# The first layer of the experts by Strassen's seven products of tiles instead of eight

## The chip, the cores and the metric
The kernel runs on one core of a Trainium2 chip. The metric is the time of the whole program on the device in microseconds (us), the median of three runs. A core has TensorE (PE; its weight loads are listed as PEld), VectorE (DVE), ScalarE (ACT), GpSimd (POOL) and SyncE (SP), which run apart and wait for each other by semaphores.

## The reference, cut to what matters
The program is one decoder layer on 64 x 256 tokens of 256 features: self-attention, cross-attention, then a block with another attention and a mixture of eight experts. The change touches the experts alone. Each takes up to a quarter of the 16384 tokens, 4096 rows:

```python
h = jax.nn.relu(jnp.einsum('ecd,edf->ecf', buf, w1) + b1[:, None, :])
y = (jnp.einsum('ecf,efd->ecd', h, w2) + b2[:, None, :]) * (1.0 - MOE_TOKEN_DROPOUT)
```

with `buf` 8 x 4096 x 256, `w1` 8 x 256 x 1024 and `w2` 8 x 1024 x 256, all in fp32. The rows of `y`, each times its gate, are added to the tokens they came from.

## The kernel before, in words
The parts of the program run one after the other: `prepare`, three calls of `attention`, `route`, `dispatch`, and `experts`, which fills the last third of the time. `experts` works in chunks of 512 rows, eight chunks to an expert and 64 in all; `k` (0 or 1) is the set of buffers of an expert, `par` (0 or 1) that of a chunk, `n` the chunk's number. There is no scheduler: each engine has its own list of instructions, written out in the source, and waits for counts of semaphores.

For a chunk, POOL gathers 512 rows from memory (`gather`, L1546), three chunks ahead. TensorE transposes them in eight pieces into two PSUM tiles `turn` (`turn_rows`, L1450), and VectorE copies these to `xT`, features on the partitions, two halves of 128 features by 512 rows (L1496). Then TensorE makes the eight tiles of the first layer: for each `f`, 128 of the 1024 hidden features, two matmuls with 512 columns, one for each half of the input features, are summed in PSUM (`hid`, two buffers, L1466). ScalarE reads each with the bias and ReLU into `hT` (L1488). After the eight tiles and the transposes of the next chunk, TensorE makes the second layer: four groups of 128 rows, each a sum of eight matmuls with 256 columns (`res`, L1476), for which a tile of `hT` is the loaded operand. VectorE scales them and adds the bias (`y`, L1532), multiplies by the gate (`gated`, L1540), and POOL adds each quarter to the output in memory by an indirect DMA (L1566), one after another: each waits until the one before it has landed.

At the first chunk of an expert VectorE waits for the weights and spreads the biases (L1511 to L1518), for which ScalarE waits (L1485). The weights of expert `e + 2` are asked for by SP when expert `e` is done (L1436).

Of the kernel before, what the change touches and what calls it, by code (L numbers as in the profile page):

```python
# [8 lines left out]
P = 128  # L9
# [1143 lines left out]
NE = 8  # L1153
# [214 lines left out]
def experts(nc, C, D, io, scratch, out):  # L1368
# [7 lines left out]
    with ExitStack() as ctx:  # L1376
# [14 lines left out]
        turn = [ps(f"turn{i}", [P, NS]) for i in range(2)]  # L1391
        hid = [ps(f"hid{i}", [P, NS]) for i in range(2)]
# [3 lines left out]
        (turned, xT_ready, hid_full, hid_read, res_full, res_read, biases, gated_ready, added, chosen, cleared, listed) = (sem(n) for n in (  # L1396
            "turned", "xT_ready", "hid_full", "hid_read", "res_full", "res_read", "biases", "gated_ready", "added", "chosen",
            "cleared", "listed"))
# [22 lines left out]
        with nc.Block() as block:  # L1421
# [20 lines left out]
            @block.tensor  # L1442
            def _(pe):
                def turn_rows(r, j, n):
                    xb, use = x_turn(r, j)
                    pe.wait_ge(x_in[xb], 64 * use + 64)
                    need(pe, xT_ready, 2 * n)
                    for a in range(2):
                        for t in range(4):
                            last = nc.tensor.transpose(turn[a][:, t * P:(t + 1) * P], x[xb][:, t, a * P:(a + 1) * P],  # L1450
                                                       C["ident_f"][:, :])
                        last.then_inc(turned, 1)

                turn_rows(0, 0, 0)
                for r in ends_apart(pe):
                    for e, k, c, par, n, j in chunks(r):
                        if c == 0:
                            pe.wait_ge(w_in[k], 48 * r + 48)
                        pe.wait_ge(xT_ready, 2 * n + 2)
                        for f in range(NF):  # L1460
                            m = NF * n + f
                            if k or c or f >= 2:
                                need(pe, hid_read, m - 1)
                            h = hid[f % 2]
                            for a in range(2):
                                last = nc.tensor.matmul(h[:, :], w1[k][:, a, f * P:(f + 1) * P], xT[par][:, a, :],  # L1466
                                                        start=a == 0, stop=a == 1)
                            last.then_inc(hid_full, 1)
                        if another(n):
                            turn_rows(r, j + 1, n + 1)  # L1470
                        pe.wait_ge(hid_read, NF * n + NF)
                        for t in range(2):
                            need(pe, res_read, 2 * n)
                            for s in range(2):
                                for f in range(NF):
                                    last = nc.tensor.matmul(res[t][:, s, :], hT[par][:, f, (2 * t + s) * P:(2 * t + s + 1) * P],  # L1476
                                                            w2[k][:, f, :], start=f == 0, stop=f == NF - 1)
                            last.then_inc(res_full, 1)

            @block.scalar  # L1480
            def _(act):
                for r in rounds(act, NE // 2):
                    for e, k, c, par, n, j in chunks(r):
                        if c == 0:
                            act.wait_ge(biases, 2 * e + 2)  # L1485
                        for f in range(NF):
                            act.wait_ge(hid_full, NF * n + f + 1)
                            nc.scalar.activation(hT[par][:, f, :], hid[f % 2][:, :], ACT.Relu, bias=b1[k][:, f:f + 1])\  # L1488
                                .then_inc(hid_read, 1)

            @block.vector
            def _(dve):
                def copy_rows(n, par):
                    for a in range(2):
                        dve.wait_ge(turned, 2 * n + a + 1)
                        nc.vector.tensor_copy(xT[par][:, a, :], turn[a][:, :]).then_inc(xT_ready, 1)  # L1496

                def list_tokens(r, j, n):
                    nc.vector.tensor_copy(token[j % (2 * XB)][:, :], C["token"][:, bass.ds(4 * n, 4)]).then_inc(listed, 1)

                for t in x:
                    nc.vector.memset(t[:, :, :], 0.0).then_inc(cleared, 1)  # L1502
                for n in range(XB - 1):
                    list_tokens(0, n, n)
                copy_rows(0, 0)
                for r in ends_apart(dve):
                    for e, k, c, par, n, j in chunks(r):
# [3 lines left out]
                        if c == 0:  # L1511
                            dve.wait_ge(w_in[k], 48 * r + 48)
                            nc.vector.tensor_copy(b1[k][:, :], C["b1"][:, bass.ds(e * NF, NF)]).then_inc(biases, 1)
                            nc.vector.tensor_copy(rank[k][:, :], C["ranks"][:, bass.ds(e, 1)])
                            for s in range(2):
                                last = nc.vector.tensor_scalar(b2s[k][:, s, :], b2[k][:, :], 0.8, None, ALU.mult)
                            last.then_inc(biases, 1)
                            dve.wait_ge(biases, 2 * e + 2)  # L1518
                        if another(n):
                            copy_rows(n + 1, 1 - par)  # L1520
                        tail = x[j % XB]
                        nc.vector.scalar_tensor_tensor(first[par][:, :, :], tail[:, :, 258:259], rank[k][:, :],
# [155 lines left out]
```

## Time and profile before
| | before |
|---|---|
| median of 3 runs | 5969.68 us (5968.39 to 5971.0) |
| the profiled execution | 5964.57 us, its span 5962.9 us |
| mean granted TensorE clock | 0.984 |
| busy share of the span: PE, PEld, DVE, ACT, POOL | 94, 68, 62, 52, 34% |

Times in the trace are counted from the span's start. A matmul in fp32 leaves two records, each with its own weight load, so the two matmuls of a tile of `hid` are four records. The end of a matmul's record is modelled and reaches past the start of the next one, so the pace of TensorE is read from start to start and not from the mean duration.

### The profile page before, as it was taken

To read this page: it belongs to the slowest core of one execution; us is meant where nothing else is said; L and a number is where in the kernel's file an instruction comes from. 1 tells how busy PE (TensorE), PEld (TensorE's weight loads), DVE (VectorE), ACT (ScalarE), POOL (GpSimd) and SP (SyncE) were. 2 spreads that over 40 slices of the span, in tenths; PEclk is the share of its full clock that TensorE was granted. 3 is DMA by queue.
4 is the path that set the end of the run, shared out by engine and by line. 5 is a ranking of instruction groups with operands and counts; after the bars stand their busy time and mean duration, and the time that the engine had idled before them with its cause. 6 is when DMAs were issued, how large, how long until landed. Compare 5 with 4: busy or idle time off the path is not lost. (4 is left out here: it accounts for less than half of the span.)

```text
span 5962.9 us, 144169 instructions
## 1 busy us (share of the span) xinstructions
PE 5621.1 (94%) x44441; PEld 4031.8 (68%) x44441; DVE 3721.2 (62%) x10169; ACT 3120.9 (52%) x6803; POOL 2036.6 (34%) x1753
## 2 busy tenths in 40 slices
PE   0999999989999999799999999958999999999998
PEld 0677777667777777577777777734666666666666
DVE  7888888778888887688888888875111111111111
ACT  4788888746666666477777777635121111211111
POOL 0322222233333333244444444401333333333332
PEclk9999999989999999999999999979999999999999
DMA  5777777556666665466766666631222222222221
GB/s 157 178 184 182 182 185 180 148 159 175 174 173 173 174 174 166 120 178 170 182 171 175 177 170 181 168 26 49 39 53 51 33 49 53 32 45 51 38 39 20
DMA packets 625511, 750.10 MB, mean 126 GB/s; under 512 B 131075, under 2 KB 554188, under 8 KB 625328
## 3 DMA queue, kind: packets, MB, share of 16 engines
q1 hardware_dynamic: 568992, 679.62, 43.7%
q0 software_dynamic: 49152, 63.10, 6.6%
q10 hardware_dynamic: 7184, 5.00, 0.3%
q8 instruction: 108, 1.77, 0.1%
q14 instruction: 75, 0.61, 0.0%
HBM read 476.49 MB, written 272.24 MB: 126 GB/s over the span
## 5 line engine op out<-in xcount | busy, mean ns | idle before, releaser
L1488 ACT ACTIVATE exp_hT<-exp_hid,exp_b 128x512 f32<-128x512 f32 x512 | 351.8, 687 | 1487.3 <-PE exp_hid L1466 1372.3
L1476 PE MATMUL exp_res<-exp_w,exp_hT 128*128 128x256 f32 x4096 | 901.2, 381 | 0.8 <-ACT exp_hT L1488 0.8
L1466 PE MATMUL exp_hid<-exp_xT,exp_w 128*128 128x512 f32 x2048 | 891.0, 593 | 0.9 <-DVE exp_xT L1496 0.9
L1476 PEld LDWEIGHTS exp_res<-exp_w,exp_hT 128*128 128x128 f32 x4096 | 773.8, 190 | 112.2 <-ACT exp_hT L1488 1.6
L1566 POOL DMA_INDIRECT out_dram<-exp_gated,exp_token x256 | 406.1, 1586 | 1099.4 <-issue 412.7
L931 DVE TENSOR_REDUCE F_tops<-F_score 128x2 f32<-128x512 f32 x1024 | 684.3, 686 | 59.8 <-PE F_score L685 40.8
L822 ACT ACTIVATE F_probs<-F_scoreT 128x512 f32<-128x512 f32 x1024 | 583.8, 590 | 236.8 <-PE F_scoreT L654 236.8
L1466 PEld LDWEIGHTS exp_hid<-exp_xT,exp_w 128*128 128x128 f32 x2048 | 389.8, 191 | 464.6 <-issue 458.5
L1496 DVE COPY exp_xT<-exp_turn 128x512 f32<-128x512 f32 x128 | 82.6, 686 | 803.2 <-PE exp_turn L1450 803.2
L931 DVE TENSOR_REDUCE A_tops<-A_score 128x3 f32<-128x384 f32 x1024 | 531.6, 554 | 62.3 <-PE A_score L671 54.0
L1532 DVE SCALAR_TENSOR_TENSOR exp_y<-exp_res,exp_b2s 128x512 f32<-128x512 f32 x128 | 88.5, 692 | 735.4 <-PE exp_res L1476 735.4
L822 ACT ACTIVATE A_probs<-A_scoreT 128x384 f32<-128x384 f32 x1024 | 451.0, 488 | 23.1 <-PE A_scoreT L642 14.7
L654 PE MATMUL F_scoreT<-QS,KS 98*128 98x256 bf16 x2048 | 365.4, 275 | 9.7 <-ACT F_probs L822 1.5
L685 PE MATMUL F_score<-KS,QS 96*128 96x256 bf16 x2048 | 362.7, 274 | 8.3 <-DMA KS<-d_k 7.4
L931 DVE TENSOR_REDUCE X_tops<-X_score 128x4 f32<-128x484 f32 x512 | 329.8, 658 | 29.0 <-PE X_score L680 28.9
L822 ACT ACTIVATE X_probs<-X_scoreT 121x512 f32<-121x512 f32 x512 | 295.1, 595 | 78.3 <-PE X_scoreT L650 72.6
L1547 POOL DMA_INDIRECT exp_x<-d_h,exp_token x256 | 269.1, 1051 | 195.6 <-DMA exp_w<-in_L_ffn_w_dram 117.9
L666 PE MATMUL A_score<-causal,ident_b 128*128 128x256 bf16 x1024 | 282.8, 276 | 12.1 <-DMA KS<-d_k 8.3
L638 PE MATMUL A_scoreT<-ident_b,causal 128*128 128x128 bf16 x2048 | 286.1, 221 | 3.2 <-ACT A_probs L822 1.1
L669 PE MATMUL A_score<-KS,QS 96*128 96x256 bf16 x1024 | 281.2, 275 | 0.0
L711 PE MATMUL F_outs<-F_probs,V 128*32 128x256 f32 x4096 | 275.4, 387 | 1.9 <-ACT F_outT L831 1.9
L642 PE MATMUL A_scoreT<-QS,KS 98*128 98x256 bf16 x1024 | 277.2, 271 | 0.0
(330 smaller groups left out, 12099.1 us busy)
## 6 DMA issues: line engine op xcount, KB each, us to landing
QS<-d_q SPq DMA_DIRECT2D x384, 192.0 KB, 3.6
KS<-d_k SPq DMA_DIRECT2D x256, 192.0 KB, 4.0
QS<-d_q SPq DMA_DIRECT2D x384, 128.0 KB, 3.9
KS<-d_k SPq DMA_DIRECT2D x256, 128.0 KB, 4.0
d_q<-A_q_parts SPq DMA_DIRECT2D x64, 384.0 KB, 3.6
d_k<-A_k_parts SPq DMA_DIRECT2D x64, 384.0 KB, 3.9
QS<-d_q SPq DMA_DIRECT2D x384, 64.0 KB, 3.7
d_q<-X_q_parts SPq DMA_DIRECT2D x64, 384.0 KB, 4.0
```

The costliest lines, as they stand in the source:

```text
L638: mm(s[:, n * P:(n + 1) * P], C["causal"][:, 0:P], ident_b[:, :], start=n == 0, stop=False, skip_group_check=True)
L642: last = mm(s[:, P:384], k[0:98, i, 0:P], q[0:98, i, :], start=False, stop=True, skip_group_check=True)
L654: last = mm(s[:, n * 256:(n + 1) * 256], k[0:98, i, n * P:(n + 1) * P], q[0:98, i, :], start=True, stop=True)
L666: mm(s[:, 0:384].rearrange("p (n k) -> p n k", n=3)[:, 0:3:2, :], ident_b[:, :], C["causal"][:, :].rearrange("p (n k) -> p n k", n=2), sta ...
L669: mm(s[:, P:384], q[0:96, i, P:256], k[0:96, i, :], start=False, stop=False, skip_group_check=True)
L685: last = mm(s[:, n * 256:(n + 1) * 256], q[0:96, i, n * P:(n + 1) * P], k[0:96, i, :], start=True, stop=True)
L822: nc.scalar.activation(probs[m % 2][0:KR, at:at + HB, :].rearrange("p u x -> p (u x)"), scoreT[i % TB][0:KR, 0:HB * TCOL], ACT.Exp)\
L931: nc.vector.tensor_reduce(dst, src, AX.X, ALU.max).then_inc(score_read, 1)
L1466: last = nc.tensor.matmul(h[:, :], w1[k][:, a, f * P:(f + 1) * P], xT[par][:, a, :], start=a == 0, stop=a == 1)
L1476: last = nc.tensor.matmul(res[t][:, s, :], hT[par][:, f, (2 * t + s) * P:(2 * t + s + 1) * P], w2[k][:, f, :], start=f == 0, stop=f == NF - 1)
L1488: nc.scalar.activation(hT[par][:, f, :], hid[f % 2][:, :], ACT.Relu, bias=b1[k][:, f:f + 1])\
L1566: nc.gpsimd.indirect_dma_start(out, bass.IndirectOffsetOnAxis(token[j % (2 * XB)][:, s:s + 1], 0), gated[par][:, s, :], None, bounds_check ...
```

## The change
The product of the first layer is cut into blocks, two by two: the weights into input half by output half (hidden features `u` and `u + 4`, in tiles of 128, for `u` from 0 to 3), the rows of the chunk into two halves of 256. Of the eight products of blocks, seven sums and differences are multiplied instead (Strassen's scheme in Winograd's form). The sums of the rows (`xTs`, `mix_rows`) are made by VectorE once a chunk, those of the weights (`w1s`, `fold_weights`) once an expert, in the last but one chunk of the expert before it, with the spreading of the biases. Each `u` then has seven matmuls with 256 columns. `lead` gets one product and later a second one on top; ScalarE copies it out after each (`lone`, `pair`). `corner` gets one. `side` gets two, one in each half of its bank, and VectorE reads both (`joined`, `side_read`) before `close` adds the last two. VectorE puts the four quarters of the two hidden tiles into `hT` by additions; ScalarE then applies bias and ReLU in place (`rectify`). The second layer's matmuls are the same 32, in an order by pairs of tiles, each with its own wait; the transposes are made in two groups of four with one `turn` buffer. PSUM holds one tile each of `turn` and `corner`, two each of `lead`, `side` and `res`. The buffers of Q, K and V, which `experts` does not use, are given back ahead of it.

```diff
+        HR, HF = NS // 2, NF // 2
+        w1s = [sb(f"w1s{i}", [P, 4, 512]) for i in range(2)]
+        xTs = [sb(f"xTs{i}", [P, 4, HR]) for i in range(2)]
+        lone, pair, both = [[sb(f"{n}{i}", [P, HR]) for i in range(2)] for n in ("lone", "pair", "both")]
+        turn = ps("turn", [P, NS])
+        lead = [ps(f"lead{i}", [P, HR]) for i in range(2)]
+        corner = ps("corner", [P, HR])
+        side = [ps(f"side{i}", [P, 2, HR]) for i in range(2)]
...
+        BY_PAIR = [f for u in range(HF) for f in (u, u + HF)]
...
+                        def close(u):
+                            s = side[u % 2]
+                            pe.wait_ge(side_read, HF * n + u + 1)
+                            mm(s[:, 0, :], ws(3, u), xT[par][:, 1, HR:NS], start=False, stop=True, skip_group_check=True)
+                            mm(s[:, 1, :], w(1, u + HF), xs(3), start=False, stop=True, skip_group_check=True).then_inc(closed, 1)
+
+                        def products(t, s, fs, begin):
+                            for f in fs:
+                                pe.wait_ge(hid_read, NF * n + BY_PAIR.index(f) + 1)
+                                last = mm(res[t][:, s, :], hT[par][:, f, (2 * t + s) * P:(2 * t + s + 1) * P], w2[k][:, f, :],
+                                          start=begin and f == fs[0], stop=f == BY_PAIR[-1], skip_group_check=True)
+                            return last
+
...
+                        for u in range(HF):
+                            l, s = lead[u % 2], side[u % 2]
+                            need(pe, pair_kept, HF * n + u - 1)
+                            mm(l[:, :], w(0, u), xT[par][:, 0, 0:HR], start=True, stop=False, skip_group_check=True)                                .then_inc(led, 1)
+                            need(pe, corner_read, HF * n + u)
+                            mm(corner[:, :], w(1, u), xT[par][:, 1, 0:HR], start=True, stop=True).then_inc(cornered, 1)
+                            if u == 0:
+                                pe.wait_ge(mixed, 4 * n + 4)
+                                if c == 0:
+                                    pe.wait_ge(folded, 4 * e + 4)
+                            need(pe, summed, 2 * HF * n + 2 * u - 2)
+                            mm(s[:, 0, :], ws(0, u), xs(0), start=True, stop=False, skip_group_check=True)
+                            mm(s[:, 1, :], ws(2, u), xs(2), start=False, stop=False, skip_group_check=True)
+                            if u:
+                                close(u - 1)
+                            pe.wait_ge(led_kept, HF * n + u + 1)
+                            mm(l[:, :], ws(1, u), xs(1), start=False, stop=True, skip_group_check=True).then_inc(sided, 1)
+                        need(pe, res_read, 2 * n)
+                        products(0, 0, BY_PAIR[0:4], True)
+                        close(HF - 1)
+                        products(0, 0, BY_PAIR[4:6], False)
                         if another(n):
+                            rows_here(r, j + 1)
+                            turn_half(j + 1, n + 1, 0)
+                        products(0, 1, BY_PAIR[0:6], False)
+                        products(0, 0, BY_PAIR[6:8], False)
+                        products(0, 1, BY_PAIR[6:8], False).then_inc(res_full, 1)
+                        if another(n):
+                            turn_half(j + 1, n + 1, 1)
+                        products(1, 0, BY_PAIR, True)
+                        products(1, 1, BY_PAIR, True).then_inc(res_full, 1)
...
+                        def rectify(u):
+                            for i in (2 * u, 2 * u + 1):
+                                f = BY_PAIR[i]
+                                act.wait_ge(summed, NF * n + i + 1)
+                                nc.scalar.activation(hT[par][:, f, :], hT[par][:, f, :], ACT.Relu, bias=b1[k][:, f:f + 1])\
+                                    .then_inc(hid_read, 1)
+                        for u in range(HF):
+                            act.wait_ge(led, HF * n + u + 1)
+                            need(act, corner_read, HF * n + u - 1)
+                            nc.scalar.activation(lone[u % 2][:, :], lead[u % 2][:, :], ACT.Copy).then_inc(led_kept, 1)
+                            if u > 1:
+                                rectify(u - 2)
+                            act.wait_ge(sided, HF * n + u + 1)
+                            need(act, summed, NF * n + 2 * u - 2)
+                            nc.scalar.activation(pair[u % 2][:, :], lead[u % 2][:, :], ACT.Copy).then_inc(pair_kept, 1)
+                        rectify(HF - 2)
+                        rectify(HF - 1)
...
+                def copy_half(n, par, a):
+                    dve.wait_ge(turned, 2 * n + a + 1)
+                    v.tensor_copy(xT[par][:, a, :], turn[:, :]).then_inc(xT_ready, 1)
+                    dve.wait_ge(xT_ready, 2 * n + 2)
+                    v.tensor_tensor(m[:, 0, :], b12, b11, ALU.subtract).then_inc(mixed, 1)
+                    v.tensor_tensor(m[:, 2, :], b22, b12, ALU.subtract).then_inc(mixed, 1)
+                    dve.wait_ge(mixed, 4 * n + 1)
+                    v.tensor_tensor(m[:, 1, :], b22, m[:, 0, :], ALU.subtract).then_inc(mixed, 1)
+                    dve.wait_ge(mixed, 4 * n + 3)
+                    v.tensor_tensor(m[:, 3, :], b21, m[:, 1, :], ALU.subtract).then_inc(mixed, 1)
+                def fold_weights(e, k, use):
+                    dve.wait_ge(w_in[k], 48 * use + 48)
+                    v.tensor_tensor(m[:, 0, :], a21, a22, ALU.add).then_inc(folded, 1)
+                    v.tensor_tensor(m[:, 2, :], a11, a21, ALU.subtract).then_inc(folded, 1)
...
+                def first_corner(n, par, u):
+                    dve.wait_ge(cornered, HF * n + u + 1)
+                    dve.wait_ge(led_kept, HF * n + u + 1)
+                    v.tensor_tensor(hT[par][:, u, 0:HR], corner[:, :], lone[u % 2][:, :], ALU.add).then_inc(corner_read, 1)
...
+                fold_weights(0, 0, 0)
+                spread_biases(0, 0)
+                copy_half(0, 0, 0)
+                copy_half(0, 0, 1)
+                mix_rows(0, 0)
+                first_corner(0, 0, 0)
...
+                        for u in range(HF):
+                            s, p, b = side[u % 2], pair[u % 2], both[u % 2]
+                            dve.wait_ge(pair_kept, HF * n + u + 1)
+                            v.tensor_tensor(b[:, :], s[:, 0, :], p[:, :], ALU.add).then_inc(joined, 1)
+                            dve.wait_ge(joined, HF * n + u + 1)
+                            v.tensor_tensor(hT[par][:, u + HF, HR:NS], s[:, 1, :], b[:, :], ALU.add).then_inc(side_read, 1)
+                            if u < HF - 1:
+                                first_corner(n, par, u + 1)
+                            dve.wait_ge(closed, HF * n + u + 1)
+                            v.tensor_tensor(hT[par][:, u, HR:NS], s[:, 0, :], p[:, :], ALU.add).then_inc(summed, 1)
+                            v.tensor_tensor(hT[par][:, u + HF, 0:HR], s[:, 1, :], p[:, :], ALU.add).then_inc(summed, 1)
                         if another(n):
+                            copy_half(n + 1, 1 - par, 0)
...
+                        if c == NC - 2 and not (k and isinstance(r, int) and r == NE // 2 - 1):
+                            fold_weights(e + 1, 1 - k, r + k)
+                            spread_biases(e + 1, 1 - k)
+                        if another(n):
+                            copy_half(n + 1, 1 - par, 1)
+                            mix_rows(n + 1, 1 - par)
+                        dve.wait_ge(biases, 2 * e + 2)
...
+                            if t == 1 and another(n):
+                                first_corner(n + 1, 1 - par, 0)
...
-            "QS": [sb(f"QS{i}", [98, H, 256], BF16) for i in range(2)],
-            "KS": [sb(f"KS{i}", [98, H * 256], BF16) for i in range(2)],
-            "V": [sb(f"V{i}", [P, 2, H, VW]) for i in range(2)], "xmean": sb("xmean", [P, 2 * B]), "xrstd": sb("xrstd", [P, 2 * B]),
...
+        with ExitStack() as stacks:
+            sb, _, _ = allocators(nc, stacks, "")
+            C["QS"] = [sb(f"QS{i}", [98, H, 256], BF16) for i in range(2)]
+            C["KS"] = [sb(f"KS{i}", [98, H * 256], BF16) for i in range(2)]
+            C["V"] = [sb(f"V{i}", [P, 2, H, VW]) for i in range(2)]
+            prepare(nc, C, D, io)
+            attention(nc, C, D, io, scratch, "A")
...
```

On TensorE one chunk before, from its first to its last matmul, is:

```order
L1466 MATMUL exp_hid<-exp_xT,exp_w 128x512 x16
L1450 MATMUL exp_turn<-ident_f,exp_x 128x128 x8
L1476 MATMUL exp_res<-exp_w,exp_hT 128x256 x32
```

Now the pair `u = 2` (its lines are alike for 1 and 3), and the first part of the second layer behind `u = 3`:

```order
L1499 MATMUL exp_lead<-exp_xT,exp_w 128x256
L1501 MATMUL exp_corner<-exp_xT,exp_w 128x256
L1507 MATMUL exp_side<-exp_xTs,exp_w1s 128x256
L1508 MATMUL exp_side<-exp_xTs,exp_w1s 128x256
L1483 MATMUL exp_side<-exp_xT,exp_w1s 128x256
L1484 MATMUL exp_side<-exp_xTs,exp_w 128x256
L1512 MATMUL exp_lead<-exp_xTs,exp_w1s 128x256
...
L1489 MATMUL exp_res<-exp_w,exp_hT 128x256 x4
L1483 MATMUL exp_side<-exp_xT,exp_w1s 128x256
L1484 MATMUL exp_side<-exp_xTs,exp_w 128x256
L1489 MATMUL exp_res<-exp_w,exp_hT 128x256 x2
```

Four other matmuls stand between L1512 of a pair and the two that close it (L1483, L1484). On VectorE nothing of the first layer stood before between two `y`; now each pair has (buffer numbers behind the names; `exp_side0` is the pair's own `side`, `corner` and `lone1` those of the pair behind it):

```order
L1619 TENSOR_TENSOR exp_both0<-exp_side0,exp_pair0 128x256
L1621 TENSOR_TENSOR exp_hT1<-exp_side0,exp_both0 128x256
L1594 REGISTER_ALU
L1596 TENSOR_TENSOR exp_hT1<-exp_corner,exp_lone1 128x256
L1625 TENSOR_TENSOR exp_hT1<-exp_side0,exp_pair0 128x256
L1626 TENSOR_TENSOR exp_hT1<-exp_side0,exp_pair0 128x256
```

The last two wait for `closed`, the first for ScalarE's copy `pair`; the next pair's L1619 stands right behind them.

## Rows read from the trace of the kernel before
**Rows 1.** The page: busy time, and the lines of the last chain.
```profile
PE 5621.1 (94%) x44441; PEld 4031.8 (68%) x44441; DVE 3721.2 (62%) x10169; ACT 3120.9 (52%) x6803; POOL 2036.6 (34%) x1753
...
PE exp_res L1476 15%; PE exp_hid L1466 15%; PE exp_turn L1450 1%; DMA out_dram<-exp_gated,exp_token 0%; DMA exp_x<-d_h,exp_token 0%; DVE exp_x L1502 0%; POOL out_dram L1566 0%; POOL exp_x L1547 0%; DVE exp_xT L1496 0%; DVE exp_y L1532 0%; ACT exp_hT L1488 0%; DVE exp_gated L1540 0%; POOLq L1547 0%; POOLq L1566 0%; POOLq L32 0%
```
**Rows 2.** One stretch of `experts`: span; busy PE, PEld, DVE, ACT, POOL; clock, DMA, GB/s.
```profile
4300.00:5900.00 1600.00, 1600.00 (x5822) 1069.61 (x5821) 261.59 (x698) 307.49 (x448) 587.29 (x446) 1.00 0.24 43
```
**Rows 3.** TensorE in order of time: start, duration, group of records.
```profile
5204.41 13.90 PE L1466 MATMUL exp_hid<-exp_xT,exp_w 128*128 128x512 f32 x32
5218.14 1.04 PE L1450 MATMUL exp_turn<-ident_f,exp_x 128*128 128x128 f32 x8
5219.09 14.08 PE L1476 MATMUL exp_res<-exp_w,exp_hT 128*128 128x256 f32 x64
5233.00 13.90 PE L1466 MATMUL exp_hid<-exp_xT,exp_w 128*128 128x512 f32 x32
```
**Rows 4.** Costliest groups: busy time, mean ns of one, idle before.
```profile
L1476 PEld LDWEIGHTS exp_res<-exp_w,exp_hT 128*128 128x128 f32 x4096 | 773.8, 190 | 112.2 <-ACT exp_hT L1488 1.6
L1488 ACT ACTIVATE exp_hT<-exp_hid,exp_b 128x512 f32<-128x512 f32 x512 | 351.8, 687 | 1487.3 <-PE exp_hid L1466 1372.3
L1532 DVE SCALAR_TENSOR_TENSOR exp_y<-exp_res,exp_b2s 128x512 f32<-128x512 f32 x128 | 88.5, 692 | 735.4 <-PE exp_res L1476 735.4
L831 ACT ACTIVATE X_outT<-X_outs 128x256 f32<-128x256 f32 x256 | 97.8, 382 | 110.6 <-PE X_outs L706 110.4
L1050 DVE TENSOR_TENSOR F_tok<-F_work,F_rec 128x256 f32<-128x256 f32 x128 | 54.3, 424 | 4.4
L1236 DVE TENSOR_TENSOR route_hit<-route_hit,route_down 128x1024 f32<-128x1024 f32 x2 | 2.4, 1224 | 0.1
```
**Rows 5.** Experts, in order of time, ScalarE, VectorE and POOL; idle before in brackets.
```profile
5204.61 0.69 DVE L1532 SCALAR_TENSOR_TENSOR exp_y<-exp_res,exp_b2s 128x512 f32<-128x512 f32 x1 [5.39 <-PE exp_res L1476]
5204.93 1.59 POOL L1566 DMA_INDIRECT out_dram<-exp_gated,exp_token  x1 [1.69 <-DMA out_dram<-exp_gated,exp_token]
5205.34 0.77 DVE L1540 TENSOR_SCALAR exp_gated<-exp_y,exp_gate 128x256 f32<-128x256 f32 x2
5206.33 0.69 ACT L1488 ACTIVATE exp_hT<-exp_hid,exp_b 128x512 f32<-128x512 f32 x1 [15.89 <-PE exp_hid L1466]
5214.34 1.59 POOL L1566 DMA_INDIRECT out_dram<-exp_gated,exp_token  x1 [1.67 <-DMA out_dram<-exp_gated,exp_token]
5228.88 1.59 POOL L1566 DMA_INDIRECT out_dram<-exp_gated,exp_token  x1 [11.59 <-issue]
```
**Rows 6.** The last chunk: ScalarE's last tile and the matmuls that wait for it.
```profile
5933.15 0.69 ACT L1488 ACTIVATE exp_hT<-exp_hid,exp_b 128x512 f32<-128x512 f32 x1 [1.03 <-PE exp_hid L1466]
5933.89 14.08 PE L1476 MATMUL exp_res<-exp_w,exp_hT 128*128 128x256 f32 x64 [0.78 <-ACT exp_hT L1488]
5941.18 0.69 DVE L1532 SCALAR_TENSOR_TENSOR exp_y<-exp_res,exp_b2s 128x512 f32<-128x512 f32 x1 [19.90 <-PE exp_res L1476]
```
**Rows 7.** Other stages: VectorE behind itself, order of time and costliest groups.
```profile
3291.43 0.26 DVE L1049 RECIPROCAL F_rec<-F_work 128x16 f32<-128x16 f32 x1 [0.61 <-PE F_work L785]
3291.72 0.42 DVE L1050 TENSOR_TENSOR F_tok<-F_work,F_rec 128x256 f32<-128x256 f32 x1
3292.06 0.68 DVE L931 TENSOR_REDUCE F_tops<-F_score 128x2 f32<-128x512 f32 x1
...
3301.47 0.18 DVE L990 BATCH_NORM_AGGREGATE F_umean_var<-F_ustats 128x2 f32<-128x6 f32 x1 [0.15 <-DVE F_ustats L986]
```
**Rows 8.** The first chunk, in order of time.
```profile
4113.33 1.97 PE L1450 MATMUL exp_turn<-ident_f,exp_x 128*128 128x128 f32 x8 [18.28 <-DMA exp_x<-d_h,exp_token]
4115.34 0.69 DVE L1496 COPY exp_xT<-exp_turn 128x512 f32<-128x512 f32 x1 [0.16 <-PE exp_turn L1450]
4116.18 15.43 PE L1466 MATMUL exp_hid<-exp_xT,exp_w 128*128 128x512 f32 x32 [0.88 <-DVE exp_xT L1496]
```
**Rows 9.** Who waited for whom in `experts`, TensorE: us in total, times, longest.
```profile
PE exp_turn L1450 <- DMA exp_x<-d_h,exp_token: 18.3, 1, 18.3
PE exp_hid L1466 <- DVE exp_xT L1496: 0.9, 1, 0.9
PE exp_res L1476 <- ACT exp_hT L1488: 0.8, 1, 0.8
```

More of the change, by code:

```diff
@@ L1443, in _, with turn_half, rows_here @@
             def _(pe):
-                def turn_rows(r, j, n):
+                mm = nc.tensor.matmul
+                def turn_half(j, n, a):
+                    need(pe, xT_ready, 2 * n + a)
+                    for t in range(4):
+                        last = nc.tensor.transpose(turn[:, t * P:(t + 1) * P], x[j % XB][:, t, a * P:(a + 1) * P],
+                                                   C["ident_f"][:, :])
+                    last.then_inc(turned, 1)
+                def rows_here(r, j):
@@ L1445, in turn_rows @@
                     xb, use = x_turn(r, j)
                     pe.wait_ge(x_in[xb], 64 * use + 64)
[L1447 to L1454, printed above, removed]
+                rows_here(0, 0)
@@ L1459, in _ @@
                         pe.wait_ge(xT_ready, 2 * n + 2)
[L1460 to L1468, printed above, removed]
@@ L1469, in _ @@
-                        if another(n):
[L1470 to L1478, printed above, removed]
+                        for u in range(HF):
[15 more added lines that the diff above has]
+                            mm(l[:, :], ws(1, u), xs(1), start=False, stop=True, skip_group_check=True).then_inc(sided, 1)
@@ L1491, in _ @@
+                        rectify(HF - 2)
+                        rectify(HF - 1)
             @block.vector
             def _(dve):
[L1493 to L1496, printed above, removed]
+                v = nc.vector
+                def copy_half(n, par, a):
+                    dve.wait_ge(turned, 2 * n + a + 1)
+                    v.tensor_copy(xT[par][:, a, :], turn[:, :]).then_inc(xT_ready, 1)
@@ new lines, in spread_biases @@
+                def spread_biases(e, k):
+                    v.tensor_copy(b1[k][:, :], C["b1"][:, bass.ds(e * NF, NF)]).then_inc(biases, 1)
+                    v.tensor_copy(rank[k][:, :], C["ranks"][:, bass.ds(e, 1)])
+                    for s in range(2):
+                        last = v.tensor_scalar(b2s[k][:, s, :], b2[k][:, :], 0.8, None, ALU.mult)
+                    last.then_inc(biases, 1)
+                def first_corner(n, par, u):
+                    dve.wait_ge(cornered, HF * n + u + 1)
+                    dve.wait_ge(led_kept, HF * n + u + 1)
+                    v.tensor_tensor(hT[par][:, u, 0:HR], corner[:, :], lone[u % 2][:, :], ALU.add).then_inc(corner_read, 1)
```

70 lines of the change are left out of this document (36 added, 34 removed).

## The prediction
> **What bounds the kernel now.** I read the page first. In its busy times TensorE leads with 94% of the span, and the chain that ended last gives 31% of the span to the experts' matmuls and 0% to everything else of that stage [rows 1]. The busy time by stretches shows TensorE busy without a gap for 1600 us of the experts, at a granted clock of 1.00, which is the 2.4 GHz level, with VectorE at 16%, ScalarE at 19% and POOL at 37% [rows 2]. The list of waits has three for TensorE in the whole stage, 20 us in sum, 18.3 of them for the first rows [rows 9]. So the experts are TensorE's stream of matmuls, and 64 chunks of 5233.00 - 5204.41 = 28.59 us [rows 3] are 1830 us of the span. What shortens the stream shortens the program, until another engine's answer comes late.
>
> The timeline gives the pace, from start to start [rows 3]. First layer: 13.73 us for 32 records, 0.429 us for one of 512 columns. Transposes: 0.95 us for eight. Second layer: 13.91 us for 64 records, 0.217 us for one of 256 columns, which holds a slower start behind the transposes; half of 0.429 is 0.2146. I take 0.216 us for a record of 256 columns and so 0.432 us for a matmul, which I call a slot below.
>
> **The change, part by part: TensorE's stream.** Removed: 16 matmuls of 512 columns, 13.73 us. Added: 28 of 256 columns, 56 records x 0.216 = 12.10 us. That is -1.63 us a chunk (-1.71 with 0.2146, -1.56 with 0.217). The columns streamed fall by an eighth, but the weight loads of the layer rise from 32 to 56. Each lasts 190 ns and there are as many in the second layer, where they fit under the 217 ns of each record [rows 3, 4]. The second layer keeps its 32 matmuls. The transposes in two groups give one more change from matmuls to transposes and back: 64 x 0.217 against 64 x 0.216 leaves some 0.1 us for such a change; I take +0.1 (0 to +0.25). Without waits a chunk is 28.59 - 1.63 + 0.10 = 27.06 us, and 64 chunks save 97.9 us.
>
> **The loop of waits in a pair.** This decides what is kept. In a pair of hidden tiles TensorE ends the second product on `lead`. Then ScalarE copies it (`pair`), VectorE makes `both`, then the quarter that frees the second half of `side`, and only then TensorE may close the pair. Its own work in between is four matmuls: 4 x 0.432 = 1.73 us. The answer takes:
> - TensorE to ScalarE: the four records of the first tile start at 5204.41, the fifth at 5204.41 + 4 x 0.429 = 5206.13, and ScalarE starts at 5206.33: 0.20 us [rows 3, 5].
> - The copy, 256 columns from PSUM: 0.382 us [rows 4].
> - ScalarE to VectorE: no row; I take the 0.05 us of ScalarE to TensorE (5933.15 + 0.69 = 5933.84 to 5933.89) [rows 6].
> - Two additions from PSUM of 256 columns at 0.424 us: 0.85 us [rows 4], and between them VectorE's wait for itself: 3291.69 to 3291.72, 0.03 us, up to 0.15 us in another row [rows 7].
> - VectorE to TensorE: 0.05 us as from ScalarE [rows 6], up to 0.15 us (4115.34 + 0.69 = 4116.03 to 4116.18) [rows 8].
> - The load of the weights, 0.19 us [rows 4], which stands behind the wait. That it counts in full shows at the end of the program: from 5933.89, 32 records of 0.216 us and the 0.20 us to the reader would give 5941.00, and `y` starts at 5941.18 [rows 6].
>
> The sum is 0.20 + 0.38 + 0.05 + 0.85 + 0.03 + 0.05 + 0.19 = 1.75 us against 1.73: late by 0.02 us, and by 0.12 with 0.15 us for the step to TensorE; with the long self-wait too, by 0.24. I take 0.06 us a pair, nearer the low end, since the 0.15 at 4116.18 was a start from idle. There are four such closings a chunk, the fourth behind four matmuls of the second layer: 4 x 0.06 x 64 = 15.4 us lost (0 to 61).
>
> **What else is late, within a pair.** Slots counted from the end of a pair's last matmul:
> - VectorE's last two additions for the pair before start at -0.43 + 0.20 = -0.23 and end by 0.62 us even when they don't overlap (F_tok ended at 3292.14 and the next instruction began at 3292.06 [rows 7]), just as `pair` arrives (0.20 + 0.38 + 0.05 = 0.63). The first matmul on `side` needs them at slot three, 0.86 us, with the load at 0.67: just in time.
> - `corner` is read at about 2.0 us and needed at 3.45. `lone` is copied from 0.63 to 1.02 and needed at 2.59.
> - VectorE has five additions, 2.12 us, in a pair's 3.02. ScalarE has two copies and two ReLUs of 512 columns, 2 x 0.38 + 2 x 0.69 = 2.14 us [rows 4]. The ReLU now reads SBUF, which I price as before.
>
> **Across the chunk.** VectorE after the last pair has the two copies of `xT` and four additions of 256 columns between buffers in SBUF. A 1024 column one takes 1.22 us [rows 4] and one from PSUM with 256 takes 0.424, so 0.42 each, 1.7 us. The second copy starts 8.9 us behind the last pair, and the sums are ready at 11.6; they are first needed at 16.7. In one chunk of eight `fold_weights` (4 x 0.69 us, as `y` with 512 columns [rows 4]) and the biases, 0.8 us, come in between: ready at 12.5. What is queued behind is `y` of the first half, due at 8.5, so POOL's first two additions to memory start up to 4 us later in the chunk. POOL's four take (5214.34 - 5204.93)/2 = 4.7 us each, 18.8 of the 27 us, and it idled 11.59 us in a chunk [rows 5]: that hides it, and TensorE needs `res` only in the next chunk's second layer. `first_corner` stands ahead of `gated` of the second half, which moves 0.6 us; the next pair's first addition comes at 2.8 us and finds VectorE free at 2.3. The 32 separate waits of the second layer are met: the last ReLU ends some 5.2 us behind the last pair, and its tile is needed at 6.6.
>
> **Start and end, once.** VectorE now folds the first weights before it copies `xT`, and with one `turn` buffer the second group of transposes waits for the first copy: the first matmul starts about 1 us later, and the sums of the rows (1.7 us) are partly covered by the first two matmuls, which run at half speed: +2 us (0 to +6). At the end the last chunk's wait of 0.8 us goes [rows 9]: -0.9. Giving back the buffers of Q, K and V issues no work on an engine: 0.
>
> **The sum.** -97.9 + 15.4 + 2.0 - 0.9 = -81.4 us. The profiled execution took 5964.57 us, so 5883.2; the median of the runs lies 5.1 us above it, and I carry that over: 5969.68 - 81.4 = 5888 us.
>
> **The rivals.** *Slower answers.* Each step of the loop could cost 0.1 us more than in the rows above, for the counts now stand in registers in most chunks and many waits are double. Then a closing is 0.2 to 0.25 us late, 51 to 64 us are lost, and the time is 5924 to 5937. For it speaks the self-wait of 0.15 us, against it the 0.05 and 0.03 us seen elsewhere [rows 6, 7].
>
> *The loop overruns: slower than before.* The same place, with VectorE's order as the mechanism: if the last two additions of the pair before end late, `both` waits behind them, the closing moves, and with it the next two additions, so that the loop feeds itself. A pair then lasts as long as VectorE's and ScalarE's whole round: seven slots plus the lateness. It decides at 97.9/256 = 0.38 us a closing. With additions at 0.55 us and steps 0.1 us longer the closing is 0.25 + 4 x 0.1 + 0.02 = 0.67 us late less what overlaps, say 0.48: 123 us lost, 25 us slower, 5996 us. Against it: 0.424 us was the mean of 128 [rows 4].
>
> *The weight loads show.* If a full load could not pass under a running matmul, 24 more loads x 0.19 = 4.6 us a chunk would be added to the -1.63: +3 x 64 = 190 us, 6160 us. Against it stand the 64 loads in 13.91 us of the second layer, where 64 x (0.217 + 0.19) would be 26 us [rows 3, 4]. The Trainium skill says just this in TensorE: Matmul & The Clock Gate, "What overlaps and what doesn't": loads overlap running matmuls only where the row group differs, and here every tile uses all rows. By that rule the result is this rival's; the trace disagrees with 190 ns loads inside a pace of 217 ns.
>
> **How the numbers follow.** Forecast (0 to 0.15 us late): 0.68, 5866 to 5912. Slower answers up to 0.3 us: 0.20, to 5950. The loop overruns: 0.06. The loads show: 0.01. The rest, 0.05, is a lateness that eats just the gain. The range is 5866 to 5930: its lower end is no lateness, -1.71 a chunk and half the switching cost (-106), the upper a lateness of 0.23 us. A measurement of this kernel tells no more than 0.2%, 12 us. Faster by more than that has 0.88 (a little of the rest too), within 0.03, slower 0.09.
>
> **What would show it right or wrong.** The page should have some 1536 more matmul records, and the start of `exp_lead` in one chunk to the next should be 27.1 to 27.6 us. TensorE's four matmuls ahead of each closing should be followed by a gap, or by none, of under 0.15 us, with the wait named VectorE's L1621. If chunks take 28 us and more, the loop of waits is wrong; if they take 27.3 and the total is not 5888, the start is.

## The result, and the profile after

The changed kernel took 5864.53 us (median of 4 runs, 5857.93 to 5866.31) against 5969.83 us (4 runs, 5968.39 to 5971.0): a ratio of 0.9821, interval 0.9808 to 0.9834, so 105.3 us or 1.8% faster. Faster was forecast, but by 81.4 us; 5864.53 lies 1.5 us below the range. The profiled execution took 5857.93 us, span 5856.2, against 5964.57: 106.6 us less, and the account below is of these two.

The page's busy times and last chain, to be read against [rows 1]:

```profile
PE 5507.3 (94%) x45977; PEld 4313.5 (74%) x45977; DVE 4335.1 (74%) x11737; ACT 3283.8 (56%) x7315; POOL 2037.6 (35%) x1753
...
PE exp_res L1489 15%; PE exp_side L1483 2%; PE exp_lead L1499 2%; PE exp_side L1484 2%; PE exp_lead L1512 2%; PE exp_corner L1501 2%; PE exp_side L1508 2%; PE exp_side L1507 2%; PE exp_turn L1457 1%; DMA out_dram<-exp_gated,exp_token 0%; DMA exp_x<-d_h,exp_token 0%; DVE exp_x L1602 0%; POOL out_dram L1682 0%; DVE exp_xT L1560 0%; DVE exp_gated L1656 0%
```

There are 45977 - 44441 = 1536 more matmul records, as forecast, and TensorE is busy 114 us less. Its matmuls are still all of the experts' part of the chain that has more than 0%; the additions went to VectorE, 614 us more, and none of them is in it. A stretch of the experts, as in [rows 2] (span; busy PE, PEld, DVE, ACT, POOL; clock, DMA share, GB/s):

```profile
4300.00:5800.00 1500.00, 1495.78 (x7136) 1311.26 (x7135) 783.77 (x2059) 446.89 (x892) 585.42 (x444) 1.00 0.26 46
```

VectorE went from 16% to 52%, ScalarE from 19% to 30%; the granted clock stayed at 1.00, the 2.4 GHz level. TensorE is idle for 4.2 us here, which it was not in [rows 2]: nearly all of it is one place, shown below. Three of the costliest groups, as in [rows 4], which had 190, 687 and 424 ns for them; only the ReLU, now from SBUF, is 25 ns dearer:

```profile
L1489 PEld LDWEIGHTS exp_res<-exp_w,exp_hT 128*128 128x128 f32 x4096 | 769.8, 190 | 97.9
L1539 ACT ACTIVATE exp_hT<-exp_hT,exp_b 128x512 f32<-128x512 f32 x512 | 339.3, 712 | 92.6 <-DVE exp_hT L1625 92.6
L1625 DVE TENSOR_TENSOR exp_hT<-exp_side,exp_pair 128x256 f32<-128x256 f32 x256 | 108.7, 425 | 263.2 <-PE exp_side L1484 263.2
```

**TensorE in one chunk**, in order of time, against [rows 3]. L1483 and L1484 are the closing:

```profile
5198.75 0.60 PE L1499 MATMUL exp_lead<-exp_xT,exp_w 128*128 128x256 f32 x2
...
5202.63 0.62 PE L1483 MATMUL exp_side<-exp_xT,exp_w1s 128*128 128x256 f32 x2
5203.09 0.60 PE L1484 MATMUL exp_side<-exp_xTs,exp_w 128*128 128x256 f32 x2
...
5203.95 0.60 PE L1499 MATMUL exp_lead<-exp_xT,exp_w 128*128 128x256 f32 x2
...
5205.68 0.60 PE L1483 MATMUL exp_side<-exp_xT,exp_w1s 128*128 128x256 f32 x2
...
5213.45 0.60 PE L1457 MATMUL exp_turn<-ident_f,exp_x 128*128 128x128 f32 x4
5213.88 4.48 PE L1489 MATMUL exp_res<-exp_w,exp_hT 128*128 128x256 f32 x20
5218.20 0.60 PE L1457 MATMUL exp_turn<-ident_f,exp_x 128*128 128x128 f32 x4
5218.64 7.07 PE L1489 MATMUL exp_res<-exp_w,exp_hT 128*128 128x256 f32 x32
5225.55 0.59 PE L1499 MATMUL exp_lead<-exp_xT,exp_w 128*128 128x256 f32 x2
```

A chunk is 5225.55 - 5198.75 = 26.80 us instead of 28.59: -1.79, where 27.1 to 27.6 us was forecast (-1.29 as the most likely). The starts are 0.43 us apart throughout, but for 0.46 behind the first closing (5202.63 to 5203.09). In the 2nd to 16th chunk that one is 0.43 too, and they take 26.78 us each. Each group of transposes takes 0.43 or 0.44 us: the two together 0.87, where the one group of before showed 0.95.

**The loop of waits**, the other engines over the same two pairs:

```profile
5201.19 0.38 ACT L1550 ACTIVATE exp_pair<-exp_lead 128x256 f32<-128x256 f32 x1 [1.35 <-PE exp_lead L1512]
5201.61 0.42 DVE L1619 TENSOR_TENSOR exp_both<-exp_side,exp_pair 128x256 f32<-128x256 f32 x1 [0.64 <-ACT exp_pair L1550]
5202.07 0.42 DVE L1621 TENSOR_TENSOR exp_hT<-exp_side,exp_both 128x256 f32<-128x256 f32 x1
5202.55 0.30 PEld L1483 LDWEIGHTS exp_side<-exp_xT,exp_w1s 128*128 128x128 f32 x2 [0.15 <-DVE exp_hT L1621]
...
5204.15 0.39 ACT L1550 ACTIVATE exp_pair<-exp_lead 128x256 f32<-128x256 f32 x1 [2.23 <-DVE exp_hT L1625]
5204.57 0.42 DVE L1619 TENSOR_TENSOR exp_both<-exp_side,exp_pair 128x256 f32<-128x256 f32 x1
5205.03 0.42 DVE L1621 TENSOR_TENSOR exp_hT<-exp_side,exp_both 128x256 f32<-128x256 f32 x1
5205.50 0.36 PEld L1483 LDWEIGHTS exp_side<-exp_xT,exp_w1s 128*128 128x128 f32 x2
```

In the second pair `lead` ends at 5203.95, the copy starts 0.20 later, lasts 0.39, and VectorE starts 0.03 behind it; its additions begin 0.46 apart, and the second ends at 5205.45, 1.50 us behind `lead`. The load starts 0.05 later, and the matmul at 5205.68 is on its slot. The first pair's copy starts 0.28 behind `lead` (5200.91), so the release comes at 5202.49, and TensorE is 0.02 to 0.03 us late. That first copy is 0.28 behind only from the 17th chunk on, where ScalarE's counts stand in registers; in the 16 before, it is 0.20 like the others. The late release shows what it costs to wait: the next group's start less a slot, 5203.09 - 0.43 = 5202.66, is 0.17 us behind the release by these rounded rows and 0.16 by the unrounded ones, and not the 0.24 of the prediction.

**The account of the 106.6 us.** 64 chunks at -1.80 us (26.78 us in most of the first 16 and 26.79 or 26.80 behind them, against 28.59) are -115.2. The experts' stage began 1.9 us later (4099.85 against 4097.99, below), behind work that the change does not touch. The first matmul of the first layer came at 4119.19 instead of 4116.18 [rows 8], 1.1 us more than that, and the first chunk, with matmuls at half clock, was 0.2 longer; the 0.8 us wait of the last chunk went. And one chunk of the 64 is 6.2 us longer than its neighbours. That sums to -115.2 + 1.9 + 1.1 + 0.2 - 0.8 + 6.2 = -106.6. The 1.9 and the 0.2 are of this one pair of executions: the profiled executions of all ten runs have the stage's start between 4097.99 and 4105.37, and two of the changed kernel's first chunk differ by 1.1 us (28.56 and 29.68). The start of the stage before, and then after:

```profile
4097.99 0.92 DVE L1502 MEMSET exp_x<- 128x1036 f32 x1 [1.23 <-PEq L84]
```
```profile
4099.85 0.92 DVE L1602 MEMSET exp_x<- 128x1036 f32 x1 [1.23 <-PEq L84]
...
4119.19 1.19 PE L1499 MATMUL exp_lead<-exp_xT,exp_w 128*128 128x256 f32 x2 [0.87 <-DVE exp_xT L1560]
```

**The long chunk** is the 33rd, in which the loop over pairs of experts jumps back, the only jump of TensorE, VectorE, POOL and SyncE. (ScalarE's loop jumps once more, at the 49th chunk, which takes the usual 26.80 us.) In order of time:

```profile
4978.16 0.65 PE L1499 MATMUL exp_lead<-exp_xT,exp_w 128*128 128x256 f32 x2
4979.24 1.17 SPq L1436 DMA_DIRECT2D exp_w<-in_L_ffn_w_dram  x2
4981.39 0.48 PE L1499 MATMUL exp_lead<-exp_xT,exp_w 128*128 128x256 f32 x1 [0.64 <-issue]
4985.70 0.17 DVE L1599 COPY exp_token<-token 128x4 int32 x1 [5.34 <-issue]
4986.75 1.22 PE L1483 MATMUL exp_side<-exp_xT,exp_w1s 128*128 128x256 f32 x2 [3.59 <-DVE exp_hT L1621]
4987.76 1.06 PE L1484 MATMUL exp_side<-exp_xTs,exp_w 128*128 128x256 f32 x2
4988.62 1.06 PE L1512 MATMUL exp_lead<-exp_xTs,exp_w1s 128*128 128x256 f32 x2
...
5011.15 0.60 PE L1499 MATMUL exp_lead<-exp_xT,exp_w 128*128 128x256 f32 x2
```

5011.15 - 4978.16 = 32.99 us. VectorE stands 5.34 us on "issue", so for nothing that the profile shows, and TensorE behind it 3.59 us; then its matmuls start 0.86 us apart (4987.76 to 4988.62) at a granted clock of 0.50 (4986.70 to 4989.40), the 1.2 GHz level, before they return to 0.43. TensorE also lost some 0.8 us of its own just before, between the two records of one matmul (the second at 4981.39). In the kernel before, the same chunk:

```profile
5032.76 3.69 PE L1466 MATMUL exp_hid<-exp_xT,exp_w 128*128 128x512 f32 x8
5033.74 0.94 SPq L1428 DMA_DIRECT2D exp_w<-in_L_ffn_w_dram  x2
5034.27 0.43 DVE L1499 COPY exp_token<-token 128x4 int32 x1
...
5061.45 1.88 PE L1466 MATMUL exp_hid<-exp_xT,exp_w 128*128 128x512 f32 x4
```

It took 28.69 us, 0.1 over its neighbours, though an expert's weights (2 MB by their shape) were issued at the same point of it. Nor does the transfer alone do it: in the changed kernel the weights are issued at the ends of five other experts too, and the chunks there take 26.8 us. What is new is a longer body, with more instructions on VectorE and the waits of the separate tiles.

### The profile page after: what moved, and what is told of

It is laid out like the page before. It is cut to its first block and busy times, and to the rows that moved or that the text cites. A ratio compares the mean times of both kernels' runs of the same rounds, so it can differ in the third digit from the quotient of the medians.

```text
span 5856.2 us, 150644 instructions
## 1 busy us (share of the span) xinstructions
PE 5507.3 (94%) x45977; PEld 4313.5 (74%) x45977; DVE 4335.1 (74%) x11737; ACT 3283.8 (56%) x7315; POOL 2037.6 (35%) x1753
## 5 line engine op out<-in xcount | busy, mean ns | idle before, releaser
L1489 PE MATMUL exp_res<-exp_w,exp_hT 128*128 128x256 f32 x4096 | 926.0, 380 | 0.0
L1545 ACT ACTIVATE exp_lone<-exp_lead 128x256 f32<-128x256 f32 x256 | 98.3, 384 | 766.5 <-PE exp_lead L1499 747.9
L1539 ACT ACTIVATE exp_hT<-exp_hT,exp_b 128x512 f32<-128x512 f32 x512 | 339.3, 712 | 92.6 <-DVE exp_hT L1625 92.6
L1625 DVE TENSOR_TENSOR exp_hT<-exp_side,exp_pair 128x256 f32<-128x256 f32 x256 | 108.7, 425 | 263.2 <-PE exp_side L1484 263.2
L1550 ACT ACTIVATE exp_pair<-exp_lead 128x256 f32<-128x256 f32 x256 | 98.2, 384 | 361.2 <-PE exp_lead L1512 223.5
```

The costliest lines, as they stand in the source:

```text
L1489: last = mm(res[t][:, s, :], hT[par][:, f, (2 * t + s) * P:(2 * t + s + 1) * P], w2[k][:, f, :], start=begin and f == fs[0], stop=f == BY_ ...
L1539: nc.scalar.activation(hT[par][:, f, :], hT[par][:, f, :], ACT.Relu, bias=b1[k][:, f:f + 1])\
```

## The experiments

All are timed against the kernel before, whose median was 5971.12 us (15 runs) beside the separate waits, the two delays and the later weights, and 5971.15 (21 runs, another chip) beside the others.

**One wait for each tile in the kernel before.** Does the second layer's start behind the transposes hide a wait for the last ReLU? Here the wait for all eight tiles is one for each.

```diff
-                        pe.wait_ge(hid_read, NF * n + NF)
...
                                 for f in range(NF):
+                                    pe.wait_ge(hid_read, NF * n + f + 1)
```

> The kernel before, with one wait ahead of each matmul of the second layer for its own tile of hT, in place of one wait for all eight ahead of the first. Theory A (hidden wait): in the kernel before the first matmul of the second layer started at 5219.09, 0.05 us behind the end of the last ReLU (5218.35 + 0.69), so a wait of some 0.19 us a chunk stood there that the list of waits does not show, and the change took it away; then a chunk falls from 28.59 to about 28.40 us and the program by 64 x 0.19 = 12 us, to about 5957 us. Theory B (the switch from transposes to matmuls itself costs that time): no change, 5969 us, 28.59 us a chunk.

Measured: 5959.37 us (11 runs), ratio 0.998, interval 0.9971 to 0.9989. TensorE, then ScalarE's last tile in this kernel:

```profile
5218.21 1.04 PE L1450 MATMUL exp_turn<-ident_f,exp_x 128*128 128x128 f32 x8
5219.08 13.98 PE L1476 MATMUL exp_res<-exp_w,exp_hT 128*128 128x256 f32 x64
5232.90 1.45 PE L1466 MATMUL exp_hid<-exp_xT,exp_w 128*128 128x512 f32 x3
```
```profile
5218.41 0.69 ACT L1488 ACTIVATE exp_hT<-exp_hid,exp_b 128x512 f32<-128x512 f32 x1 [1.03 <-PE exp_hid L1466]
```

Eight transposes in one group take 0.87 us, and the second layer 13.82. In [rows 3] it was 0.95 and 13.91: 0.17 us, and 64 x 0.17 = 11 us of the 11.8 measured. So the slow start was a wait, and two groups of transposes cost no more than one. The list of waits [rows 9] has 0.8 us for it, of the last chunk alone. The 0.19 us a chunk and 5957 us expected were near.

**Halves of the matmul in the kernel before.** What do the weight loads cost by themselves? The first layer's matmuls of 512 columns become two of 256, 64 loads instead of 32.

```diff
+                            for half in range(2):
+                                cols = slice(half * 256, half * 256 + 256)
                                 for a in range(2):
-                                last = nc.tensor.matmul(h[:, :], ..., xT[par][:, a, :], ...)
+                                    last = nc.tensor.matmul(h[:, cols], ..., xT[par][:, a, cols], ...)
```

> The kernel before, with each first-layer matmul of 512 columns as two of 256, so 32 matmuls and 64 weight loads in place of 16 and 32, all eight products and no new wait. It is the price of the narrower matmuls alone. Theory A (loads of 190 ns pass under a matmul record of 216 ns): 64 x 0.216 = 13.82 us in place of 13.73, +0.09 a chunk, 6 us, 5976. Theory B (the added loads show in full): 32 x 0.19 = 6.1 us a chunk, +389 us. The last ReLU may start a little later or earlier; within 0.05 us a chunk.

Measured: 5978.28 us (10 runs), ratio 1.0014, interval 1.0005 to 1.0023. TensorE in it:

```profile
5211.58 13.98 PE L1468 MATMUL exp_hid<-exp_xT,exp_w 128*128 128x256 f32 x64
5225.39 1.04 PE L1450 MATMUL exp_turn<-ident_f,exp_x 128*128 128x128 f32 x8
5226.34 14.08 PE L1478 MATMUL exp_res<-exp_w,exp_hT 128*128 128x256 f32 x64
```

The first layer takes 13.81 us instead of 13.73, 0.2158 us for a record. 32 more loads cost 0.08 us a chunk (5 of the 7.1 us between the medians), not 32 x 0.19 = 6.1: the rival in which the loads show is dead.

**The buffers alone.** The kernel before with only the release of Q, K and V.

```diff
-            "QS": [sb(f"QS{i}", [98, H, 256], BF16) for i in range(2)],
...
+        with ExitStack() as stacks:
+            sb, _, _ = allocators(nc, stacks, "")
+            C["QS"] = [sb(f"QS{i}", [98, H, 256], BF16) for i in range(2)]
...
```

> The kernel before with the second part of the change alone: the buffers of Q, K and V are given back ahead of the experts. Theory A: nothing is issued, no difference, 5970 us within 0.1%. Theory B (the places of the experts' buffers in SBUF matter to a load or a transfer): a chunk of another length than 28.59 us.

Measured: 5969.98 us (10 runs), ratio 0.9998, interval 0.9988 to 1.0007; a chunk is 28.59 us. It costs and gives nothing.

**A delay in the loop of waits of the changed kernel.** How far is each closing from late? An addition whose result nobody reads goes between VectorE's two, of 4 columns and, in a second kernel, of 256. The edit shown is that of 4 columns; both kernels also have the buffer `spare`.

```diff
                             dve.wait_ge(joined, HF * n + u + 1)
+                            v.tensor_tensor(spare[:, 0:4], b[:, 0:4], p[:, 0:4], ALU.add)
                             v.tensor_tensor(hT[par][:, u + HF, HR:NS], s[:, 1, :], b[:, :], ALU.add).then_inc(side_read, 1)
```

> The changed kernel, with one more addition of 4 columns on VectorE, into a buffer nobody reads, between the two additions that free side. It adds some 0.13 us to the loop of waits. Theory A (a margin of about 0.09 us in the second to fourth closing, none in the first): 0.13 + 3 x 0.04 = 0.25 us a chunk, 16 us, 5880. Theory B (the load of weights counts in full, no margin anywhere): 4 x 0.13 x 64 = 33 us, 5898. Theory C (wide margin): under 9 us, only the first closing pays.

> The changed kernel, with one more addition of 256 columns on VectorE at the same place, some 0.34 us. Theory A (margin 0.09): 0.34 + 3 x 0.25 = 1.09 us a chunk, 70 us, 5934, so a chunk near 27.9 us. Theory B (no margin): 4 x 0.34 x 64 = 87 us, 5951. If VectorE's later additions are pushed into the next pair's as well, the loss feeds itself and a pair is later by more than 0.34: over 100 us.

Measured: 5865.5 us (4 runs), ratio 0.9823, interval 0.9808 to 0.9838, and 5936.43 us (4 runs), ratio 0.9943, interval 0.9928 to 0.9959. Chunks are 26.88 and 27.93 us. The small one adds 0.08 us (5213.23 to 5213.31) where 0.13 was expected, and only the first closing pays it: +0.08 a chunk from the 17th on, and 0.01 in the first 16. So it is no larger than the slack that it was to measure. The median does not show the 4 us this should make (5865.5 against 5864.53 and, on another chip, 5863.52). The kernel with 256 columns, VectorE and TensorE:

```profile
5201.44 0.42 DVE L1620 TENSOR_TENSOR exp_both<-exp_side,exp_pair 128x256 f32<-128x256 f32 x1
5201.90 0.42 DVE L1622 TENSOR_TENSOR exp_spare<-exp_both,exp_pair 128x256 f32<-128x256 f32 x1
5202.24 0.41 DVE L1623 TENSOR_TENSOR exp_hT<-exp_side,exp_both 128x256 f32<-128x256 f32 x1
5202.71 0.70 PE L1484 MATMUL exp_side<-exp_xT,exp_w1s 128*128 128x256 f32 x2
5203.25 0.59 PE L1485 MATMUL exp_side<-exp_xTs,exp_w 128*128 128x256 f32 x2
```

The delay is 0.34 us, and a chunk grows by 1.13 = 0.34 + 3 x 0.26: the first closing had no slack, the other three 0.08 us each. In the first 16 chunks, where no closing was late, it grows by 1.06 = 4 x 0.265. It takes 64 x 1.13 = 72 us, as measured (5936.43 - 5864.53). The release at 5202.65 and the next group at 5203.25 give 5203.25 - 0.43 - 5202.65 = 0.17 us again from release to stream, 0.16 unrounded, and so at every closing of this kernel. This is also the rival of slower answers, made on purpose.

**The weights later at the jump.** Does the long chunk come from the transfer that runs as the loop jumps? In the changed kernel SyncE issues the weights of each later expert only when VectorE has made the first addition (`both`) of the next chunk's fourth pair; at the jump that is 13.5 us further into the chunk.

```diff
                             sp.wait_ge(res_read, 2 * n + 2)
+                            sp.wait_ge(joined, HF * n + HF + 4)
                             weights(e + 2, k)
```

> The changed kernel, with SP asking for the next expert's weights only when VectorE has done the first additions of the fourth pair of the next chunk, some 10 us later. Theory A (VectorE's instructions behind the loop's branch are late because the 2.1 MB of weights are moved at that moment): the 5.3 us in which VectorE has no instruction at the branch go, the distance of 59.79 us over two chunks there becomes 53.6, and the program is 5 to 6 us faster than the changed kernel, about 5858. Theory B (the longer loop body costs this whatever else is moved): the gap stays, about 5864.5.

Measured: 5856.22 us (5 runs), ratio 0.9808, interval 0.9794 to 0.9821. The long chunk in it:

```profile
4981.31 0.66 PE L1500 MATMUL exp_lead<-exp_xT,exp_w 128*128 128x256 f32 x2
...
4984.91 0.48 PE L1500 MATMUL exp_lead<-exp_xT,exp_w 128*128 128x256 f32 x1 [1.00 <-issue]
4986.20 0.38 DVE L1600 COPY exp_token<-token 128x4 int32 x1 [2.68 <-issue]
4987.25 0.70 PE L1484 MATMUL exp_side<-exp_xT,exp_w1s 128*128 128x256 f32 x2 [0.56 <-DVE exp_hT L1622]
4987.79 0.59 PE L1485 MATMUL exp_side<-exp_xTs,exp_w 128*128 128x256 f32 x2
...
4995.93 1.15 SPq L1436 DMA_DIRECT2D exp_w<-in_L_ffn_w_dram  x2
...
5010.25 0.59 PE L1500 MATMUL exp_lead<-exp_xT,exp_w 128*128 128x256 f32 x2
```

28.94 us instead of 32.99, VectorE's wait 2.68 instead of 5.34, and TensorE goes on at 0.43 us a matmul behind its stop (0.59 us groups from 4987.79), not at 0.86. So 4.1 of the 6.2 us came with the transfer at the jump, not the 5 to 6 expected; 2.1 us stay with the jump of this longer body, and what of the body causes them was not tried. Nor is it shown how the transfer delays an engine whose rows name no wait for it. The profile lists two DMA queues named `instruction` on the same DMA engines (0.11 MB from 4960 to 4995 in the changed kernel), so that late instructions are a candidate, which no run separates.

**Both once more, side by side on another chip**, the changed kernel and the one with the later weights.

> The changed kernel once more, on the chip of the next run, for a comparison with it: 5864 us, chunks of 26.8 us, one of them 6 us longer at the loop's branch.

> The changed kernel with the weights asked for later, once more beside the changed kernel itself. Theory A (the transfer held up the instructions): 4 us less than the changed kernel, from 6.2 to 2.1 us at the branch; the rest of the 8 us seen between medians is between chips. Theory B: all 8 us are real and sit elsewhere too.

Measured: 5863.52 us (5 runs, 5858.33 to 5865.61; ratio 0.9816, interval 0.9803 to 0.983) and 5855.35 us (5 runs, 5851.1 to 5859.3; ratio 0.9806, interval 0.9793 to 0.982). The jump costs 6.7 and 2.1 us here (0.2 of each in the chunk ahead of the long one). The later weights are the fastest version, by 8 us in medians both times, but the intervals of the two ratios overlap, and the traces give the edit 4 to 5 of them: 4.1 at the jump in the first pair of profiled executions, 4.6 in the second. The second pair differs by 8.2 us in all, and the other 3.5 stand where the edit had not yet moved anything: the stage began 1.3 us earlier (4101.66 against 4102.96), the first matmul came 0.8 us sooner behind it, and the first chunk took 28.23 instead of 29.68 us. In the first pair these places went the other way, by 3.2 us. So the expectation of 4 us fits, and that all 8 are the edit's is not borne out.

## Why the prediction was right and wrong

Right: TensorE's stream sets the time, and a matmul of 256 columns takes 0.432 us, so 28 of them in place of 13.73 us give -1.63 us (the halves show 0.2158 us for a record, -1.65). The loop of waits is what decides what is kept, and its steps up to VectorE's release were priced within 0.02 us (1.50 us against 1.51). The start (+1.3 for +2) and the end (-0.8 for -0.9) held. The release of the buffers is nothing. The loads do not show: loads of 190 ns kept a pace of 216 ns here and in the halves. By the rule of the Trainium skill (TensorE: Matmul & The Clock Gate, "What overlaps and what doesn't"), that loads overlap running matmuls only where row groups differ, they would have shown; these traces disagree with it.

Wrong, in order of size:
- **The step that failed is "The transposes in two groups give one more change ... I take +0.1".** I read the 0.1 us over 64 x 0.216 as a price of changing between transposes and matmuls. It was a wait. The ReLU of the last tile, in the kernel before:

```profile
5218.35 0.69 ACT L1488 ACTIVATE exp_hT<-exp_hid,exp_b 128x512 f32<-128x512 f32 x1 [1.03 <-PE exp_hid L1466]
```

It ends at 5219.04. The matmuls could have started at 5218.14 + 0.87 = 5219.01; counted back from the next chunk they ran from 5233.00 - 13.82 = 5219.18 on, 0.17 us later. The one-wait-each kernel takes this away and gains 0.17 us a chunk; the changed kernel takes it away too, by its separate waits. So the term is -0.17 instead of +0.10: 64 x 0.27 = 17 us. The ReLU's end could have been read beside [rows 3]; I relied on [rows 9], where the wait is missing.
- **"The load of the weights, 0.19 us ... counts in full"** was too dear. From a release to TensorE's stream it is 0.16 us (after the first closing, and at all four with the long delay), not 0.05 + 0.19 = 0.24. The last chunk, from which I took it, was TensorE's start from 0.78 us of rest [rows 6]. The loop's sum is 1.50 + 0.16 = 1.66 against 1.73 us, so a closing has 0.07 us to spare (0.07 to 0.08 by the long delay), and only the first, in 48 of the 64 chunks, is late by 0.02, since its copy starts 0.08 later than the others. That is all there is of the rival of slower answers with its counts in registers. Lost is 0.02 x 48 = 1 us and not 15.4, of which 5 were the sum (1.75 against 1.73) and 10 an allowance for a step of 0.15 us that did not come: 14.4 us.
- **Not foreseen: the jump of the loop, 6.2 us** in one chunk, that went the other way. 4.1 of it came with the transfer of the weights.

From -81.4 the transposes make -17.3, the closings -14.4, the jump +6.2, the later start of the stage +1.9, the start and first chunk -0.7, the end +0.1 and the slot (-1.645 instead of -1.63 us a chunk) -1.0: -106.6, as seen. So the forecast was nearer than its terms, by luck: two terms that were not in it, the jump and the later start of the stage, took back 8 us.

The lower end of the range allowed only for a cheaper switch and no lateness, and had no case in which the change takes away a wait that was there. It was also added up wrongly: 64 x (-1.71 + 0.05) = -106.2, and with the +2.0 of the start and the -0.9 of the end -105.1, so 5864.6 and not 5866 us. That the measured 5864.53 lies on it would be luck too, since that end stands for chunks of 26.93 us and not 26.80.

## What to carry to other kernels

A start that is slow by a tenth of a microsecond in every round of a loop is worth an account of its own: put the last release beside it before calling it overhead, since the list of waits can be silent on it. Here one line, a wait for each tile, gave 11.8 us, a ninth of the gain, without any of the change. Where a loop of waits closes within a tenth of the work that covers it, a change is to be bounded on both sides, and a deliberate delay in the loop, longer than the slack, measures it in one run. When a loop's body grows, look at the one round in which it jumps, and keep large transfers away from it. Before a few microseconds between two medians are credited to an edit, look in the traces whether they stand behind the first place that it touches.

## What the runs showed of the hardware

- A wait of TensorE of 0.17 us in every chunk stood in no list, since a group of matmuls is drawn past its end (13.90 us long where the next starts after 13.73 [rows 3]).
- From the end of the VectorE instruction that TensorE waits for to TensorE's running stream 0.16 us pass (0.17 by the rounded rows), though a weight load alone lasts 0.19; behind a rest of 0.78 us it was 5941.18 - 0.20 - 6.91 - 5933.84 = 0.23 us [rows 6].
- ScalarE's copy began 0.20 us behind TensorE's last matmul on `lead`, and 0.28 us in the first pair of every chunk from the 17th on, where its counts stand in registers.
- At its loop's only jump VectorE stood 5.34 us with the weights' transfer under way and 2.68 us with it issued later (5.33 and 2.33 in the repeats), and behind a stop of TensorE of 3.59 us matmuls came 0.86 us apart at a granted clock of 0.50, the 1.2 GHz level.
